# Parted PSUM ring, mixed couples of scores and maxima, and value products by pairs of heads in an attention between two expert layers

## The chip, the cores and the metric

One core of a Trainium2 chip runs the whole program in one launch. The metric is the device time of a run in microseconds (us). Three timed runs of the kernel before gave 1308.31, 1308.95 and 1309.26 us, median 1308.95. The profile is of one further execution.

## The reference, cut to what matters

```python
x = L0_attn_x                                    # (4, 1024, 128) fp32
x = x + 0.5 * ffn(layernorm(x))                  # 8 experts, the best 2 for each of 4096 tokens
x = x + attn(layernorm(x))
x = x + 0.5 * ffn(layernorm(x))                  # the same experts and router

def attn(x):                                     # 16 heads of 8 features; one projection for q, k and v
    qkv = (x @ W_qkv.T).reshape(b, n, 16, 8).transpose(0, 2, 1, 3)
    score = softmax(einsum('bhif,bhjf->bhij', qkv, qkv) / sqrt(8))
    return einsum('bhij,bhjf->bihf', score, qkv).reshape(b, n, 128) @ W_o.T

def ffn(x):                                      # router in fp32, top 2 of 8, softmax over the two gates
    return sum over experts of gate * (clip(x1 * silu(x2)) @ Wo + bo)
```

## The kernel before, in words

There are three stages: the first expert layer, the attention, and the second expert layer. The change lies in the attention alone.

**Tiling.** The attention works through 16 teams: 4 batches by 4 groups of four heads (`TEAM`). A team has two halves of 512 queries each. A half has 8 key tiles of 128 (one key tile of four heads is a unit). A slot is one head, one key tile and 512 queries: its score product fills one PSUM bank (128 keys by 512 queries, fp32). There are 1024 slots, issued in 512 couples. The two scores of a couple contract over 64 rows each, the first over partitions 0 to 63, the second over 64 to 127, so the two can run beside each other in TensorE.

**Row maxima.** Before a half's scores can be made, its row maxima must be known, because they are part of the operands. A maxima unit `n` is two products of 62 rows by 512 keys (a low one on partitions 0 to 61, a high one from partition 64), each into a bank, and one VectorE reduction over both banks. There are 512 such units. The first 18 (`MAX_FIRST`) come before the first score; after that each couple brings one unit, 18 units ahead of the scores. The last 18 couples have none.

**Exponentials.** ScalarE turns each score bank into `att_probs` (8 slots of SBUF).

**Value products.** All value products of a half accumulate in bank 7, cut into four strips of 32 partitions, one for each head of the team. `tensor_values(n, part)` multiplies unit `n` (four heads) with 256 of the 512 queries: four matmuls on the four strips, which the trace shows as eight (fp32). Couple `slot` issues half of the products of unit `slot // 4 - 1`. Part 0 waits until the exponential of the last slot of its unit is done, which is the slot just before the couple.

**PSUM.** Banks 0 to 6 are one ring (class `Ring`): scores (one bank), maxima units (two banks) and the chores' banks take the next free place in the order of issue, and each waits until the holder seven banks back has been read. A maxima unit whose banks are 6 and 0 is not contiguous and is reduced by two instructions (line 1975) in place of one (line 1970).

**Chores.** Everything else of the attention stage is a list of chores by slot, with an order written out by hand (lines 598 to 670). All engines go through the same list: after the couple's own work, each engine does its part of the couple's chores. The chores are: `place` (the maxima's transpose, 31 in the list and one before), `finish` (at a half's end ScalarE copies bank 7 to `att_o_t`, TensorE transposes it, ScalarE copies it back, VectorE takes reciprocals of the sums and GpSimd multiplies), `rows` (the output projection, every fourth team), `prepare` (the next batch's operands) and `route` (the router of the second expert layer). 110 of their steps take a bank, in 102 couples; eight of these couples have two.

**Order on TensorE.** A couple is: first score (line 2264), second score (2268), low maxima (2247), high maxima (2248), value products (2286), chores. The loop is in `tensor_attention`. On VectorE it is: maxima reduction, chores; on ScalarE: two exponentials, chores.

## Time and profile before

| what | us |
|---|---|
| median of three timed runs | 1308.95 |
| the profiled execution's own time | 1308.1 |
| its span, first to last instruction | 1306.4 |
| first expert layer, until the first maxima product | 0 to 335.5 |
| first score to the last exponential | 363.6 to 1060.0 |
| PE busy in the span | 1150.1 |
| VectorE (DVE) busy in the span | 1126.8 |
| ScalarE (ACT) busy in the span | 887.6 |
| GpSimd (POOL) busy in the span | 482.2 |

PE is TensorE's matmul side and PEld its weight loads, which overlap. A matmul's end is modelled, so starts are the safer readings on PE: two matmuls on different rows of the array start within hundredths of a microsecond of each other. "Idle before" is the time an engine stood still ahead of an instruction, and the name behind the arrow is who ended it.

### The profile page before, as it was taken

How to read it: one execution, taken by the hardware profiler on the slowest of the kernel's cores; microseconds unless marked ns; L12 is line 12 of the kernel's file. 1: busy time of each engine (PE TensorE's matmuls, PEld its weight loads, DVE VectorE, ACT ScalarE, POOL GpSimd, SP SyncE). 2: the span in 40 equal slices, each digit the busy share in tenths (PEclk: the TensorE clock that was granted, in tenths of full speed). 3: DMA queues.
4: the chain of work that ended last, by engine and by line, in shares of the span. 5: the costliest groups of instructions: out<-in, count | busy, mean ns of one | idle time of the engine just before them, and what ended most of it. 6: DMA issues, size and time to landing. Idle time of an engine off the chain costs nothing.

```text
span 1306.4 us, 27214 instructions
## 1 busy us (share of the span) xinstructions
PE 1150.1 (88%) x9031; PEld 630.4 (48%) x9031; DVE 1126.8 (86%) x2337; ACT 887.6 (68%) x1879; POOL 482.2 (37%) x545
## 2 busy tenths in 40 slices
PE   3847999888589999999999999999998889999993
PEld 2746888777123223223323223233322258788882
DVE  7877888877899999989998999999999368988885
ACT  1223555555168999898888888898887965455651
POOL 3873547334113000324235313333333117543232
PEclk9999999999679999999999999999999999999997
DMA  8124665564010200002001010001000503554654
GB/s 277 50 70 171 215 212 187 206 215 134 29 50 19 67 6 15 18 18 63 5 27 37 11 32 19 18 26 28 18 5 24 181 31 138 191 204 181 247 199 139
DMA packets 58617, 123.55 MB, mean 95 GB/s; under 512 B 12352, under 2 KB 33826, under 8 KB 58448
## 3 DMA queue, kind: packets, MB, share of 16 engines
q1 hardware_dynamic: 49488, 103.83, 23.1%
q0 software_dynamic: 8704, 16.93, 4.1%
q8 instruction: 75, 1.23, 0.4%
q10 hardware_dynamic: 288, 1.05, 0.2%
q14 instruction: 62, 0.51, 0.1%
HBM read 36.66 MB, written 23.88 MB: 46 GB/s over the span
## 4 chain that ended last, share of the span: by engine, by line
PE 56%; DVE 25%; issue 5%; POOL 5%; ACT 5%; DMA 3%; SPq 1%; DVEq 0%; POOLq 0%; ACTq 0%
PE psum L2286 14%; DVE att_neg_part L1970 12%; PE psum L2264 8%; PE psum L2200 8%; PE psum L2188 7%; PE psum L2190 7%; PE psum L2247 5%; POOL rows_dram L1263 4%; DVE att_neg_part L1975 2%; DMA ffn_block_rows<-rows_dram 2%; DVE ffn_x2c L1911 2%; DVE stats L1604 2%; ACT att_probs L1456 2%; DVE ffn_hidden L1922 1%; PE psum L2309 1%
## 5 line engine op out<-in xcount | busy, mean ns | idle before, releaser
L1456 ACT ACTIVATE att_probs<-psum 128x512 f32<-128x512 f32 x1024 | 554.9, 599 | 59.3 <-PE psum L2268 31.2
L1970 DVE TENSOR_REDUCE att_neg_part<-psum 128x2 f32<-128x1024 f32 x443 | 519.1, 1216 | 33.3 <-PE psum L2248 31.6
L2286 PE MATMUL psum<-att_probs,att_values 128*16 128x256 f32 x4096 | 322.1, 386 | 12.4 <-ACT att_o_t L1471 7.7
L1424 ACT ACTIVATE ffn_silu<-ffn_x2c,ffn_rec 128x256 f32<-128x256 f32 (+1 forms) x320 | 154.6, 487 | 170.1 <-DVE ffn_x2c L1911 170.0
L1279 POOL DMA_INDIRECT y_dram<-ffn_y,ffn_block_rows x144 | 142.4, 989 | 235.0 <-ACT ffn_y L1442 206.5
L2268 PE MATMUL psum<-att_right,att_left 64*128 64x512 f16 x512 | 199.5, 390 | 17.3 <-DVE att_neg_part L1970 13.2
L2247 PE MATMUL psum<-att_right,att_left 62*128 62x512 f16 x512 | 198.4, 388 | 15.6 <-DVE att_neg_part L1970 10.1
L2264 PE MATMUL psum<-att_right,att_left 64*128 64x512 f16 x512 | 199.5, 390 | 8.5 <-DVE att_neg_part L1970 6.8
L2248 PE MATMUL psum<-att_right,att_left 62*128 62x512 f16 x512 | 200.0, 391 | 0.0
L1911 DVE TENSOR_SCALAR ffn_x2c<-psum,ffn_rec 128x256 f32<-128x256 f32 (+1 forms) x320 | 162.8, 513 | 36.7 <-PE psum L2190 33.0
L2188 PE MATMUL psum<-ffn_block_t,ffn_rec 128*128 128x256 f32 (+1 forms) x640 | 179.0, 362 | 1.2 <-ACT ffn_block_t L1375 1.2
L2190 PE MATMUL psum<-ffn_block_t,ffn_rec 128*128 128x256 f32 (+1 forms) x640 | 178.2, 360 | 0.0
L1263 POOL DMA_INDIRECT rows_dram<-rows,place_i x128 | 127.5, 996 | 122.6 <-PE psum L2268 53.6
L2286 PEld LDWEIGHTS psum<-att_probs,att_values 128*16 128x16 f32 x4096 | 69.4, 94 | 192.7 <-issue 134.6
L1922 DVE SCALAR_TENSOR_TENSOR ffn_hidden<-psum,ffn_rec,ffn_silu 128x256 f32<-128x256 f32 (+1 forms) x320 | 144.4, 451 | 19.0 <-ACT ffn_silu L1424 17.0
L2200 PE MATMUL psum<-ffn_hidden,ffn_rec 128*128 128x256 f32 (+1 forms) x640 | 140.6, 363 | 11.8 <-DVE ffn_hidden L1930 11.6
L2264 PEld LDWEIGHTS psum<-att_right,att_left 64*128 64x128 f16 x512 | 47.3, 92 | 203.7 <-ACT att_probs L1456 128.6
L2200 PEld LDWEIGHTS psum<-ffn_hidden,ffn_rec 128*128 128x128 f32 x640 | 111.0, 190 | 32.4 <-DVE ffn_hidden L1930 19.8
L2190 PEld LDWEIGHTS psum<-ffn_block_t,ffn_rec 128*128 128x128 f32 x640 | 117.6, 192 | 13.6
L2188 PEld LDWEIGHTS psum<-ffn_block_t,ffn_rec 128*128 128x128 f32 x640 | 111.9, 192 | 12.2 <-ACT ffn_block_t L1375 1.8
L1192 POOL TENSOR_TENSOR att_attn<-att_o_t,att_inv_sum 128x128 f32<-128x128 f32 x30 | 12.1, 404 | 227.7 <-DVE att_inv_sum L1999 213.0
L1975 DVE TENSOR_REDUCE att_neg_part<-psum 128x1 f32<-128x512 f32 x138 | 88.3, 681 | 4.3 <-PE psum L2248 3.6
(238 smaller groups left out, 1176.6 us busy)
## 6 DMA issues: line engine op xcount, KB each, us to landing
ffn_rec<-record SPq DMA_DIRECT2D x80, 776.5 KB, 3.9
ffn_block_rows<-rows_dram SPq DMA_DIRECT2D x64, 130.0 KB, 3.1
record<-in_L_ffn_W SPq DMA_DIRECT2D x16, 256.0 KB, 6.5
att_left<-q_parts_dram SPq DMA_DIRECT2D x64, 64.0 KB, 2.2
y_dram<-ffn_y,ffn_block_rows POOLq DMA_INDIRECT x144
x_sb<-in_L_attn_x SPq DMA_DIRECT2D x4, 512.0 KB, 7.0
record<-in_L_ffn_Wo SPq DMA_DIRECT2D x8, 256.0 KB, 7.2
rows_dram<-rows,place_i POOLq DMA_INDIRECT x128, 2.4
```

The lines of the kernel that those rows point to most:

```text
L1263: G.indirect_dma_start(rows_dram[k_ffn][:, :], bass.IndirectOffsetOnAxis(ap=r.place_i[:, k, t:t + 1], axis=0), r.rows[:, t, k, :], None).t ...
L1456: S.activation(probs[:, slot % PROBS, :], ring_bank(("score", slot))[:, :], ACT.Exp, scale=unlift).then_inc(att_bank.by_act, 1)
L1911: V.tensor_scalar(mix[k].x2c[:, n % 2, few], chunk_bank[n % 4][:, few], mix[k].rec[:, s, CLIP_LO + c:CLIP_LO + c + 1], mix[k].rec[:, s, CL ...
L1970: last = V.tensor_reduce(out=neg_part[:, h % 2, keys, p::PAIR, t], in_=psum[:, low:high + 1, :], axis=AX.X, op=ALU.max, negate=True)
L2188: TE.matmul(both[:, few], mix[k].rec[:, s, W2 + c * P:W2 + (c + 1) * P], mix[k].block_t[:, m % 2, few], start=True, stop=True)
L2190: TE.matmul(both[:, w1_few], mix[k].rec[:, s, W1 + c * P:W1 + (c + 1) * P], mix[k].block_t[:, m % 2, few], start=True, stop=True).then_inc ...
L2200: last = TE.matmul(y_bank[n % 2][:, few], mix[k].rec[:, s, WO + c * F:WO + (c + 1) * F], mix[k].hidden[:, n % 2, c, few], start=(c == 0), ...
L2247: TE.matmul(bank[low], left[s][PRODUCTS[0], p, q], right[s][PRODUCTS[0], p, k], start=True, stop=True)
L2248: TE.matmul(bank[high], left[s][PRODUCTS[1], p, q], right[s][PRODUCTS[1], p, k], start=True, stop=True).then_inc(maxed, 1)
L2264: TE.matmul(low, left[s][WITH_MAX[0], p, k], right[s][WITH_MAX[0], p, q], start=True, stop=True).then_inc(att_bank.filled, 1)
L2268: TE.matmul(high, left[s][WITH_MAX[1], p, k], right[s][WITH_MAX[1], p, q], start=True, stop=True).then_inc(att_bank.filled, 1)
L2286: last = TE.matmul(value_bank[head * VS:head * VS + VW, q], values[:, b % 2, kt, team * TEAM + head, :], probs[:, (UNIT * n + j) % PROBS, ...
```

## The change

Three things change together in the attention.

1. The ring of seven banks becomes two: banks 0 to 3 for maxima units (two units), banks 4 to 6 for scores and chores. Every maxima unit is contiguous, so line 1975's form is gone.
2. A couple on TensorE becomes: first score, high maxima, low maxima, second score, value products, chores.
3. Value products go by pairs of slots. Pair `m` is slots `2m` and `2m + 1`. It multiplies two heads with all 512 queries: the four strips now hold (odd or even query tile) by (head of the pair), and the bank's two halves of columns hold the two pairs of the team. It is issued in couple `2m + 4` (`VALUE_LAG` = 2). The number of matmuls, and the 256 columns of each, are the same; the moving operand is two runs of 128 columns in place of one of 256. The last multiply of `finish` becomes two, because the layout of the sums has changed.

```diff
-        return (self.at[name] + k) % self.banks
+        return self.first + (self.at[name] + k) % self.banks
...
-        att_bank = Ring(7, semaphore("bank_full"), semaphore("bank_emptied"), maxed, reduced)
+        MAX_BANKS = 2 * PAIR
+        max_bank = Ring(0, MAX_BANKS, None, None, maxed, reduced)
+        att_bank = Ring(MAX_BANKS, 7 - MAX_BANKS, semaphore("bank_full"), semaphore("bank_emptied"), None, None)
...
-                o = o_t[:, half, :].rearrange("p (t j d) -> p t j d", t=HT, j=TEAM)
-                G.tensor_tensor(attn_of(i, half), o[:, :, :, 0:DH],
-                                inv_sum[:, :, :].unsqueeze(3).to_broadcast([P, HT, TEAM, DH]),
-                                ALU.mult).then_inc(finished, 1)
+                o = sums_of(half)
+                for j in range(PAIR):
+                    last = G.tensor_tensor(attn_of(i, half, j), o[:, j, :, :, 0:DH], inverse_of_sums(j), ALU.mult)
+                last.then_inc(finished, 1)
...
-                    if slot >= PROBS and slot % UNIT == 0:
-                        S.wait_ge(valued, slot // UNIT - PROBS // UNIT + 1)
+                    if slot >= PROBS and slot % PAIR == 0:
+                        S.wait_ge(valued, (slot - PROBS) // PAIR + 1)
...
-            if high == low + 1:
-                last = V.tensor_reduce(out=neg_part[:, h % 2, keys, p::PAIR, t], in_=psum[:, low:high + 1, :],
-                                       axis=AX.X, op=ALU.max, negate=True)
-            else:
-
-                for k, where in enumerate((low, high)):
-                    last = V.tensor_reduce(out=neg_part[:, h % 2, keys, PAIR * k + p, t:t + 1], in_=bank[where],
-                                           axis=AX.X, op=ALU.max, negate=True)
-            last.then_inc(reduced, 1)
+            V.tensor_reduce(out=neg_part[:, h % 2, keys, p::PAIR, t], in_=psum[:, low:high + 1, :],
+                            axis=AX.X, op=ALU.max, negate=True).then_inc(reduced, 1)
...
-                tensor_scores(slot)
-                for n in max_units(slot + 1):
-                    tensor_row_max(n)
-                if slot >= UNIT:
-                    tensor_values(slot // UNIT - 1, slot % UNIT // 2)
+                tensor_scores(slot, max_units(slot + 1))
+                if slot // PAIR >= VALUE_LAG:
+                    tensor_values(slot // PAIR - VALUE_LAG)
                 for chore in chores[slot] + chores[slot + 1]:
                     tensor_chore(*chore)
-            for part in range(2):
-                tensor_values(NSCORES // UNIT - 1, part)
+            for m in range(NSCORES // PAIR - VALUE_LAG, NSCORES // PAIR):
+                tensor_values(m)
...
             TE.matmul(low, left[s][WITH_MAX[0], p, k], right[s][WITH_MAX[0], p, q],
                       start=True, stop=True).then_inc(att_bank.filled, 1)
+            for n in beside:
+                tensor_row_max(n, (1, 0))
             for emptied in att_bank.empty_before(("score", slot + 1)):
                 TE.wait_ge(*emptied)
...
-            q = slice(part * HALF // 2, (part + 1) * HALF // 2)
-            for j, head in enumerate(HEAD_OF):
-                last = TE.matmul(value_bank[head * VS:head * VS + VW, q], values[:, b % 2, kt, team * TEAM + head, :],
-                                 probs[:, (UNIT * n + j) % PROBS, q],
-                                 start=(kt == 0 and part == 0), stop=(kt == BT - 1 and part == 1))
-            if part == 1:
-                last.then_inc(valued, 1)
+            TE.wait_ge(*att_bank.emptied(("score", PAIR * m + 1)))
+            for odd in range(2):
+                for h in range(PAIR):
+                    g = odd * PAIR + h
+                    queries = probs[:, (PAIR * m + h) % PROBS, :].rearrange("p (c o q) -> p c o q", o=2, q=P)[:, :, odd, :]
+                    last = TE.matmul(value_bank[g * VS:g * VS + VW, p * HALF // 2:(p + 1) * HALF // 2],
+                                     values[:, b % 2, kt, team * TEAM + HEAD_OF[PAIR * p + h], :], queries,
+                                     start=(kt == 0 and p == 0), stop=(kt == BT - 1 and p == 1))
+            last.then_inc(valued, 1)
```

## Rows read from the trace of the kernel before

**Rows 1.** Windows: span, PE, PEld, DVE, ACT, POOL busy, clock, DMA.
```profile
363.00:1024.00 661.00, 624.58 (x6178) 200.09 (x6178) 620.68 (x875) 580.88 (x1137) 200.97 (x230) 0.99 0.09 25
```
**Rows 2.** Page, costliest groups: busy and mean ns, then idle before.
```profile
L1970 DVE TENSOR_REDUCE att_neg_part<-psum 128x2 f32<-128x1024 f32 x443 | 519.1, 1216 | 33.3 <-PE psum L2248 31.6
...
L1192 POOL TENSOR_TENSOR att_attn<-att_o_t,att_inv_sum 128x128 f32<-128x128 f32 x30 | 12.1, 404 | 227.7 <-DVE att_inv_sum L1999 213.0
L1975 DVE TENSOR_REDUCE att_neg_part<-psum 128x1 f32<-128x512 f32 x138 | 88.3, 681 | 4.3 <-PE psum L2248 3.6
```
**Rows 3.** Waits of DVE and of PE, 363 to 1024: us, times, longest.
```profile
DVE att_neg_part L1970 <- PE psum L2248: 29.9, 51, 1.1
DVE att_neg_part L1975 <- PE psum L2248: 3.6, 6, 1.0
...
PE psum L2286 <- ACT att_o_t L1471: 6.9, 20, 0.5
```
**Rows 4.** Timeline of DVE over one plain half: start, us, what.
```profile
456.52 1.23 DVE L1970 TENSOR_REDUCE att_neg_part<-psum 128x2 f32<-128x1024 f32 x1 [0.45 <-PE psum L2248]
...
459.11 1.28 DVE L1975 TENSOR_REDUCE att_neg_part<-psum 128x1 f32<-128x512 f32 x2
460.31 4.61 DVE L1970 TENSOR_REDUCE att_neg_part<-psum 128x2 f32<-128x1024 f32 x4
464.83 1.28 DVE L1975 TENSOR_REDUCE att_neg_part<-psum 128x1 f32<-128x512 f32 x2
466.02 6.88 DVE L1970 TENSOR_REDUCE att_neg_part<-psum 128x2 f32<-128x1024 f32 x6
472.81 1.29 DVE L1975 TENSOR_REDUCE att_neg_part<-psum 128x1 f32<-128x512 f32 x2
```
**Rows 5.** Timeline of PE over one couple late in that half.
```profile
467.28 0.39 PE L2264 MATMUL psum<-att_right,att_left 64*128 64x512 f16 x1
...
467.30 0.39 PE L2268 MATMUL psum<-att_right,att_left 64*128 64x512 f16 x1
...
467.50 0.38 PE L2247 MATMUL psum<-att_right,att_left 62*128 62x512 f16 x1
...
467.83 0.62 PE L2286 MATMUL psum<-att_probs,att_values 128*16 128x256 f32 x8
...
468.39 0.39 PE L2264 MATMUL psum<-att_right,att_left 64*128 64x512 f16 x1
```
**Rows 6.** Timeline of ACT and PE over a half's end.
```profile
452.94 0.59 ACT L1471 COPY att_o_t<-psum 128x512 f32<-128x512 f32 x1
...
453.63 0.62 PE L2286 MATMUL psum<-att_probs,att_values 128*16 128x256 f32 x8 [0.38 <-ACT att_o_t L1471]
...
455.28 0.66 PE L2309 MATMUL psum<-identity,att_o_t 128*128 128x128 f32 x4
...
455.87 0.39 PE L2264 MATMUL psum<-att_right,att_left 64*128 64x512 f16 x1
...
455.97 0.59 ACT L1476 COPY att_o_t<-psum 128x512 f32<-128x512 f32 x1 [0.28 <-PE psum L2309]
```
**Rows 7.** Timeline around a couple with two chores.
```profile
518.30 0.59 ACT L1483 COPY att_xh_t<-psum 128x512 f32<-128x512 f32 x1 [0.28 <-PE psum L2315]
...
518.30 0.39 PE L2264 MATMUL psum<-att_right,att_left 64*128 64x512 f16 x1
...
518.89 0.37 PE L2247 MATMUL psum<-att_right,att_left 62*128 62x512 f16 x1 [0.20 <-ACT att_xh_t L1483]
...
519.32 1.23 DVE L1970 TENSOR_REDUCE att_neg_part<-psum 128x2 f32<-128x1024 f32 x1 [0.57 <-PE psum L2248]
```
**Rows 8.** Timeline of ACT: half ends, the last half without maxima.
```profile
472.05 0.59 ACT L1471 COPY att_o_t<-psum 128x512 f32<-128x512 f32 x1
...
1019.03 0.59 ACT L1471 COPY att_o_t<-psum 128x512 f32<-128x512 f32 x1
...
1037.77 0.59 ACT L1471 COPY att_o_t<-psum 128x512 f32<-128x512 f32 x1
```

More of the change, by code:

```diff
@@ L55, with __init__ @@
 class Ring:
-    def __init__(self, banks, filled, by_act, maxed, reduced):
-        self.banks = banks
+    def __init__(self, first, banks, filled, by_act, maxed, reduced):
+        self.first, self.banks = first, banks
         self.filled, self.by_act, self.maxed, self.reduced = filled, by_act, maxed, reduced
@@ L591, in max_banks @@
         def max_banks(n):
-            return [att_bank.bank(("max", n), k) for k in range(PAIR)]
+            return [max_bank.bank(("max", n), k) for k in range(PAIR)]
         PLACINGS = 2 * NTEAM
@@ L1467, in scalar_chore @@
                 i, half = which
-                S.wait_ge(valued, i * UNITS + (half + 1) * BT)
+                S.wait_ge(valued, i * PAIRS + (half + 1) * PAIRS // 2)
                 if i:
@@ L1998, in vector_chore @@
                         V.wait_ge(finished, 2 * i + half)
-                    V.reciprocal(inv_sum[:, :, :], o[:, :, :, DH]).then_inc(sums_inverted, 1)
+                    V.reciprocal(inv_sum[:, :], all_sums(half)).then_inc(sums_inverted, 1)
                 else:
                     V.wait_ge(finished, 2 * i + half)
-                    settle(V.reciprocal(inv_sum[:, :, :], o[:, :, :, DH]))
-                    V.tensor_tensor(attn_of(i, half), o[:, :, :, 0:DH],
-                                    inv_sum[:, :, :].unsqueeze(3).to_broadcast([P, HT, TEAM, DH]),
-                                    ALU.mult).then_inc(finished, 1)
+                    settle(V.reciprocal(inv_sum[:, :], all_sums(half)))
+                    for j in range(PAIR):
+                        last = V.tensor_tensor(attn_of(i, half, j), o[:, j, :, :, 0:DH], inverse_of_sums(j), ALU.mult)
+                    last.then_inc(finished, 1)
             elif what == "rows" and step == 2 and which[0] == B - 1:
@@ L2014, in vector_chore, with attn_of, sums_of, all_sums @@
                 vector_prepare(which, step, part)
-        def attn_of(i, half):
+        def attn_of(i, half, j):
             team = i % TEAMS
             where = attn[:, half * HT:(half + 1) * HT, team * TEAM * DH:(team + 1) * TEAM * DH]
-            return where.rearrange("p t (j d) -> p t j d", j=TEAM)
+            return where.rearrange("p t (h j d) -> p j t h d", h=PAIR, j=PAIR)[:, j, :, :, :]
+        def sums_of(half):
+            return o_t[:, half, :].rearrange("p (j t h d) -> p j t h d", j=PAIR, t=HT, h=PAIR)
+        def all_sums(half):
+            return o_t[:, half, :].rearrange("p (s d) -> p s d", d=VS)[:, :, DH]
+        def inverse_of_sums(j):
+            sums = inv_sum[:, :].rearrange("p (j t h) -> p j t h", j=PAIR, t=HT)[:, j, :, :]
+            return sums.unsqueeze(3).to_broadcast([P, HT, PAIR, DH])
         def vector_prepare(b, step, part):
@@ L2241, in tensor_row_max, with tensor_max_half, tensor_scores @@
                 TE.wait_ge(rights_in[s], rights_before(i))
-            for emptied in att_bank.empty_before(("max", n)):
+            for emptied in max_bank.empty_before(("max", n)):
                 TE.wait_ge(*emptied)
-            low, high = max_banks(n)
-            q = slice((g * HT + t) * P, (g * HT + t + 1) * P)
-            k = slice(keys * HALF, (keys + 1) * HALF)
-            TE.matmul(bank[low], left[s][PRODUCTS[0], p, q], right[s][PRODUCTS[0], p, k], start=True, stop=True)
-            TE.matmul(bank[high], left[s][PRODUCTS[1], p, q], right[s][PRODUCTS[1], p, k],
-                      start=True, stop=True).then_inc(maxed, 1)
-        def tensor_scores(slot):
+            for k in halves:
+                tensor_max_half(n, k, k == halves[-1])
+        def tensor_max_half(n, k, whole):
+            i, g, p, t, keys = max_of(n)
+            s = i % OPERANDS
+            q = slice((g * HT + t) * P, (g * HT + t + 1) * P)
+            seen = slice(keys * HALF, (keys + 1) * HALF)
+            product = TE.matmul(bank[max_banks(n)[k]], left[s][PRODUCTS[k], p, q], right[s][PRODUCTS[k], p, seen],
+                                start=True, stop=True)
+            if whole:
+                product.then_inc(maxed, 1)
+        def tensor_scores(slot, beside):
             i, at = divmod(slot, TURN)
@@ L2269, in tensor_scores, with tensor_values @@
                       start=True, stop=True).then_inc(att_bank.filled, 1)
-        def tensor_values(n, part):
+        def tensor_values(m):
+            n, p = divmod(m, UNIT // PAIR)
             i, u = divmod(n, UNITS)
@@ L2275, in tensor_values @@
             b, team = divmod(i, TEAMS)
-            if part == 0:
+            if p == 0:
                 TE.wait_ge(*when_emptied(("prepare", b, 15)))
```

15 lines of the change are left out of this document (8 added, 7 removed).

## The prediction
> **What bounds the kernel now.** I read the windows by stage first. From the first score to the last maxima reduction (363 to 1024 us) the span is 661.0 us, and DVE is busy for 620.7 of them, PE for 624.6 and ACT for 580.9 [rows 1]. PE's figure contains modelled ends, so it says little; DVE's is 94% and ends are real. The waits of DVE in the same stretch say where most of the other 40.3 us are: 29.9 + 3.6 = 33.5 us in 57 waits, all of them for the high maxima product, line 2248 [rows 3]. So DVE is the bound, and what it loses it loses to TensorE being late with a maxima unit.
>
> The timeline of a plain half (no `rows`, `prepare` or `route`) shows how close the engines stand. Sixteen couples go from one copy of bank 7 at 452.94 [rows 6] to the next at 472.05 [rows 8]: 19.11 us. DVE's reductions follow each other without a gap but for one wait of 0.45 us [rows 4]. Four contiguous ones take 464.83 - 460.31 = 4.52 us, so 1.13 us each; six take 472.81 - 466.02 = 6.79, again 1.13. A split unit takes 460.31 - 459.11 = 1.20 or 466.02 - 464.83 = 1.19.
>
> PE is nearly as full. In one couple the second score starts at 467.30, the low maxima at 467.50, the value products at 467.83, the next first score at 468.39 [rows 5]. From score to value products is 0.53, from there to the next score 0.56, so PE needs 0.53 + 0.56 = 1.09 to 1.10 us for a couple, 0.03 less than DVE. The last half has no maxima, and there the same copies are 1037.77 - 1019.03 = 18.74 us apart [rows 8]: that is what ACT and PE allow when DVE asks for nothing. A perfect decoupling would so win 19.11 - 18.74 = 0.37 us in a plain half.
>
> Where does the one wait of a half come from? PE's value products wait for the copy of bank 7, which ends at 452.94 + 0.59 = 453.53 (call it Tc), and start at 453.63. Then PE runs without a pause: a couple, the transposes at 455.28, and the score of the couple after that at 455.87, Tc + 2.34 [rows 6]. Its maxima are ready for DVE at 456.52, Tc + 2.99 [rows 4]. DVE had a little less than two units in hand, and PE has spent 0.46 on the copy and 0.59 on the transposes. It is TensorE's own work that is late, not its waits for exponentials: among PE's waits in the stretch the value products are held 6.9 us by the copy [rows 3], and no wait of comparable size for `att_probs` stands beside it.
>
> **The change part by part.**
>
> *Contiguous maxima.* 138 / 2 = 69 of the 512 units are split [rows 2]. Each saves 1.195 - 1.13 = 0.065 us on DVE (by busy time, 2 x 0.681 - 1.216 = 0.146, but neighbours overlap at their ends, so the spacing of starts is the price): 69 x 0.065 = 4.5 us. This lies on the engine that sets the pace. The part of it that falls just ahead of a wait only makes that wait longer. With 33.5 us of waits in 57 places, I count 85% as kept: -3.8 us. Bounds: 0 (all swallowed) and -10.1 (0.146 each).
>
> *Two rings, maxima.* By the lines of `empty_before`, a unit's banks needed before: the reduction of the unit two back and, for the second bank, the exponential of slot - 2. Now they need the reduction two back only. But the first score, which stands ahead of them on TensorE in both kernels, needs the exponential of slot - 3 in both. So in DVE's pace nothing moves: reduction two back ends, + 0.15 the second score started before (467.15 to 467.30, the ends being 466.02 + 1.13 k) [rows 4, 5], and now the high maxima does. The second row group is then free 0.20 later for the second score, and the value products follow at the same + 0.68. After Tc, too, the low maxima is the second pair in either order, 0.2 after the first score: DVE's Tc + 2.99 stays. Cost 0, gain 0.
>
> *Two rings, chores.* Eight couples take two chore banks; in the couple behind them a maxima unit had to wait for the reduction just before it: it starts at 518.89, and DVE stood idle for 0.57 us [rows 7]. This goes. What is late next is the second score: with three banks it needs the bank of the first chore, whose copy ends at 518.30 + 0.59 = 518.89. It would have come at 518.30 + 0.2 = 518.5, and starts near 518.97. So DVE gets its unit 0.37 earlier, but the value products behind the second score come 0.07 later (0.2 + 0.1 of order and latency against what the low maxima needed before), and the next unit with them. Net +0.07 x 8 = +0.6. Bounds: +0.45 each (3.6 us, if PE had no wait there before) and -0.57 each (-4.6).
> A single chore holds one of three banks. Behind a `finish`, the first score two couples on needs the copy that ends at 455.97 + 0.59 = 456.56, and TensorE comes to it at 455.87 + 1.10 = 456.97 [rows 6]: 0.4 to spare, less the 0.1 that a release takes. Cost 0 in the 94 couples with one chore; if that cover is gone, PE loses what is missing each time.
>
> *Order within a couple.* The pairs still use opposite row groups (0 to 63 beside 64 to 127), so I take the same spacing of 0.20 to 0.22 between pairs. The trace of before has no pair of score and maxima side by side. Bounds: 0 and +0.2 per pair, which is the full start-to-start time when nothing overlaps [rows 5].
> The Trainium skill (TensorE: Matmul & The Clock Gate, Part 3, "What overlaps and what doesn't") says that a weight load overlaps a running matmul only where the row group differs. The new order alternates low, high, low, high as the old one did, so by that page too the sum has 0 here; no run so far shows a mixed pair.
>
> *Value products.* Eight matmuls of 256 columns on four strips, as before. They wait for exponentials of slot - 3 and older in place of slot - 1; that frees TensorE where ACT is late, but such waits are not in the list [rows 3]. The wait for the copy of bank 7 is in the same couple (last pair of a half in couple at + 2, first of the next in at + 4). Gain 0 to -2. The moving operand in two runs has no row; I take 0.56 as before. Bounds: 0 and a doubled 0.56, which would be the end of any gain.
> The Trainium skill (PSUM — Partial Sum Buffer, Specifications) says that any non-contiguous access pattern slows matmuls. It speaks of PSUM, where the output stays one run of 256; were it to hold for what is read, this change would be the slower one. No run so far shows it.
>
> *Last pairs, finish.* At the very end half of the last products no longer waits for the last exponential, but the copy after it stands behind a table load on ACT: 0. GpSimd's second multiply adds at most 0.40 us in each of 30 `finish` chores, and GpSimd sat idle 227.7 us ahead of them [rows 2]: 0. ACT's wait for old values is relaxed: 0. No DMA moves. The 18 couples at the end lose the bank reserve of seven, but are paced by ACT, and TensorE is freer: -0.3.
>
> **Sum.** -3.8 + 0.6 - 0.3 = -3.5 us. The profiled execution took 1308.1 us (its span of 1306.4 and 1.7 around it), so 1304.6 for such an execution. The median of the timed runs is 0.85 higher: 1308.95 - 3.5 = 1305.4 us.
>
> **The rivals.**
>
> A, DVE's waits shrink. If the looser order (value products two pairs behind, maxima ahead of the second score) lets TensorE build up a lead, each half falls from DVE's pace to the 18.74 of ACT: 0.37 x 28 halves = 10.4 us, 1308.95 - 10.4 = 1298.5. For it: DVE waits for PE alone, in 57 places. Against it: in those places PE is shown working without a pause, and a lead grows by 0.03 us a couple at most.
>
> B, slower: a score waits for a chore's copy. With three banks the chore's bank comes round in the second couple. The reserve I computed is 0.3 to 0.4 us behind a `finish`. It decides from the point where the copy ends over 0.3 us later against TensorE than in [rows 6]; then PE, with only 0.03 us of slack a couple, hands it on to DVE. At 0.1 us in each of the 94 couples and the full 0.45 in the eight doubles: 9.4 + 3.6 - 3.8 = +9.2, 1318.2 us; half of that is 1313.
>
> C, slower: TensorE's couple gets longer, through the mixed pairs or the two-run reads. The point is 0.03 us a couple; every 0.01 beyond costs 494 x 0.01 = 4.9 us. At +0.05 it would be +10 - 3.8, some 1315; with one pair not overlapping (+0.2) it would be 1308.95 + 494 x 0.17 = 1393.
>
> D, nothing shows: the 4.5 us of splits end in front of waits, 1308.
>
> **How the numbers follow.** The forecast gets 0.44 (its own range 1303 to 1307.5), A 0.20, B 0.14, C 0.09, D 0.13. What a measurement here can tell from no change is about 0.2%, 2.6 us, so faster means below 1306.3. The forecast lies below that in about 0.31 of its 0.44, and the rest is no change. Faster: 0.31 + 0.20 = 0.51; same: 0.13 + 0.13 = 0.26; slower: 0.14 + 0.09 = 0.23. The range leaves out the upper part of B and C and the lower part of A: 1296 to 1312.
>
> **What would show it.** Line 1975's form is gone, 512 reductions, DVE busy in the stretch down by 5 to 10 us. A plain half takes 18.9 to 19.0 us between copies of bank 7, with one wait of DVE of 0.4 to 0.5. The 0.57 behind double chores is gone, and the wait after it is longer. Value products show 0.56 to the next first score. The forecast is wrong if DVE's waits for line 2247 or 2248 fall well under 30 us in total (A), if scores wait for ACT's chore copies in more than the eight places (B), or if a couple on PE without waits takes over 1.13 us (C).

## The result, and the profile after

The changed kernel takes 1300.68 us (median of 4 runs, 1299.04 to 1302.95) beside 1308.97 us for the kernel before in the same session: a ratio of 0.9947, interval 0.9933 to 0.9961. Timed again in a later session (the last run below) the ratio was 0.9955, interval 0.9942 to 0.9968, or -6.0 us. Faster by 6 to 8 us, then, where -3.5 was forecast: 1300.68 lies in the stated range of 1296 to 1312, which holds "no change" as well, and 4.7 us under the forecast.

The page and the windows of the changed kernel first. They answer to [rows 1, 2]: there is one form of reduction, 512 times, and the busy time of all of them is 594.7 us where 519.1 + 88.3 = 607.4 stood. The last reduction starts at 1017.12 us where it started at 1023.91. DVE is busy for 616.7 us up to 1018, for 620.7 up to 1024 before: 4 us less, where 5 to 10 were foretold.

```profile
L1973 DVE TENSOR_REDUCE att_neg_part<-psum 128x2 f32<-128x1024 f32 x512 | 594.7, 1213 | 35.5 <-PE psum L2259 32.1
```
```profile
363.00:1018.00 655.00, 625.01 (x6190) 175.82 (x6188) 616.74 (x809) 580.79 (x1138) 205.53 (x261) 0.99 0.09 25
```

The waits of DVE and PE in that stretch (total us, times, longest) answer to [rows 3]. In this kernel line 2259 is both maxima products, 2277 the first score, 2283 the second, 2304 the value products, 1475 the copy of bank 7. DVE still waits for nothing but maxima: 30.4 us in 47 places for 33.5 in 57 (30.8 in 48 in the second profile of this kernel, below). PE's 6.5 us ahead of the value products are its stands for the copy.

```profile
DVE att_neg_part L1973 <- PE psum L2259: 30.4, 47, 1.4
```
```profile
PE psum L2304 <- issue: 6.5, 19, 0.4
```

DVE over a plain half (timeline: start, us, what), as in [rows 4]. Fourteen reductions run without a split, 1.13 apart, and the one wait is what it was, 0.46.

```profile
456.44 15.93 DVE L1973 TENSOR_REDUCE att_neg_part<-psum 128x2 f32<-128x1024 f32 x14
472.82 1.23 DVE L1973 TENSOR_REDUCE att_neg_part<-psum 128x2 f32<-128x1024 f32 x1 [0.46 <-PE psum L2259]
```

PE and ACT late in that half and over its end, as in [rows 5, 6]. The pair of a score and a maxima product starts within 0.04 us, the next pair 0.23 later. Behind the copy of bank 7 the value products stand 0.31 for the copy; then PE runs a couple in 470.50 to 471.59 = 1.09 us, and reaches the score behind the transposes at 472.18, the copy's end (469.84) + 2.34. That is to the hundredth what [rows 6] have.

```profile
463.33 0.39 PE L2277 MATMUL psum<-att_right,att_left 64*128 64x512 f16 x1
463.37 0.56 PE L2259 MATMUL psum<-att_right,att_left 62*128 62x512 f16 x2
463.60 0.38 PE L2283 MATMUL psum<-att_right,att_left 64*128 64x512 f16 x1
463.90 0.63 PE L2304 MATMUL psum<-att_probs,att_values 128*16 128x256 f32 x8
...
469.25 0.59 ACT L1475 COPY att_o_t<-psum 128x512 f32<-128x512 f32 x1
...
469.94 0.62 PE L2304 MATMUL psum<-att_probs,att_values 128*16 128x256 f32 x8 [0.31 <-issue]
470.50 0.39 PE L2277 MATMUL psum<-att_right,att_left 64*128 64x512 f16 x1
...
471.04 0.62 PE L2304 MATMUL psum<-att_probs,att_values 128*16 128x256 f32 x8
471.59 0.66 PE L2326 MATMUL psum<-identity,att_o_t 128*128 128x128 f32 x4
472.18 0.39 PE L2277 MATMUL psum<-att_right,att_left 64*128 64x512 f16 x1
```

Behind two chores, as in [rows 7]: the maxima start beside the first score, the second score stands 0.64 us behind it for the chore's copy, and DVE has one wait of 1.37.

```profile
515.20 0.39 PE L2277 MATMUL psum<-att_right,att_left 64*128 64x512 f16 x1
515.21 0.60 PE L2259 MATMUL psum<-att_right,att_left 62*128 62x512 f16 x2
...
515.84 0.39 PE L2283 MATMUL psum<-att_right,att_left 64*128 64x512 f16 x1
...
518.44 1.23 DVE L1973 TENSOR_REDUCE att_neg_part<-psum 128x2 f32<-128x1024 f32 x1 [1.37 <-PE psum L2259]
```

What the chores cost DVE is read from starts. In the changed kernel the three units ahead of the wait begin at 513.36, and the unit behind it at 518.44: 5.08 us.

```profile
513.36 3.71 DVE L1973 TENSOR_REDUCE att_neg_part<-psum 128x2 f32<-128x1024 f32 x3
```

In the kernel before, the same three units and both waits take from 516.39 to 521.51, 5.12 us (the wait of [rows 7] lies inside).

```profile
516.39 2.35 DVE L1970 TENSOR_REDUCE att_neg_part<-psum 128x2 f32<-128x1024 f32 x2
...
521.51 1.23 DVE L1970 TENSOR_REDUCE att_neg_part<-psum 128x2 f32<-128x1024 f32 x1 [0.96 <-PE psum L2248]
```

ACT in the last half without maxima, as in [rows 8], and under it the row of the kernel before that is needed beside it: the half takes 17.76 us (the copy before stands at 1012.25) for 18.74, because 20 exponentials take 10.11 us for 10.85.

```profile
1020.03 10.11 ACT L1460 ACTIVATE att_probs<-psum 128x512 f32<-128x512 f32 x20
1030.01 0.61 ACT L1475 COPY att_o_t<-psum 128x512 f32<-128x512 f32 x1
```
```profile
1027.04 10.85 ACT L1456 ACTIVATE att_probs<-psum 128x512 f32<-128x512 f32 x20
```

**A ruler.** ACT copies bank 7 once in each half, 32 times. The starts of these copies cut the attention into 31 pieces that can be compared between kernels to hundredths. In the table: start of the first copy, the 29 halves behind it, the last two (which have no maxima, or few), and one plain half (the fifth).

| kernel | first copy | 29 halves | last two | plain half |
|---|---|---|---|---|
| before | 388.81 | 630.22 | 42.35 | 19.11 |
| after | 386.82 | 625.43 | 40.87 | 18.97 |
| after, again | 388.35 | 625.52 | 40.59 | 18.97 |
| value products alone | 388.58 | 628.76 | 39.73 | 19.11 |
| parted rings alone | 388.35 | 631.01 | 42.62 | 19.25 |
| parted rings, mixed order | 387.41 | 627.37 | 42.62 | 18.97 |
| after, with splits | 387.79 | 627.45 | 40.50 | 19.10 |

Between first and last copy the change is worth 672.57 - 666.30 = 6.3 us (6.5 in the second profile): 4.8 (4.7) in the 29 halves, 1.5 (1.8) in the last two. The first copy is another matter: the two profiles of the same changed kernel have it 2.0 and 0.5 us earlier than before. Part of that lies ahead of the attention, where the kernels do not differ: the first maxima product starts at 335.48 us before, at 335.21 and 336.14 in the two profiles after. From it to the first copy it is 53.33 us before, 51.61 and 52.21 after. In this stretch the granted clock differs too. In the windows of 368 to 372 us (column ahead of the last two) it is 0.50, which is the 1.2 GHz level, for the whole window before and in the second profile, and it rises within the window in the first. In the next 4 us it is 0.73 before, 0.92 in the second profile and 1.00 in the first.

```profile
368.00:372.00 4.00, 4.00 (x25) 0.56 (x24) 3.26 (x3) 1.97 (x4) 0.00 (x0) 0.50 0.00 0
```
```profile
368.00:372.00 4.00, 4.00 (x35) 0.69 (x36) 3.05 (x4) 2.54 (x6) 0.00 (x0) 0.67 0.00 0
```
```profile
368.00:372.00 4.00, 4.00 (x25) 0.56 (x23) 3.19 (x4) 2.96 (x6) 0.00 (x0) 0.50 0.00 0
```

So of the 8.3 us between the first two medians some 6.4 are the change in the middle of the kernel. The rest is not shown to be the change's. Some of it differs from one execution to the next; whether the new order also shortens the start cannot be told from the clock's part in it, with one profile of the kernel before.

### The profile page after: what moved, and what is told of

The parts are those of the page before. It is cut to its first block, busy times and chain, and to the rows that moved or that the text cites. A ratio compares the mean times of both kernels' runs of the same rounds, so it can differ in the third digit from the quotient of the medians.

```text
span 1297.3 us, 26926 instructions
## 1 busy us (share of the span) xinstructions
PE 1152.7 (89%) x9031; PEld 607.3 (47%) x9031; DVE 1122.0 (86%) x2270; ACT 886.0 (68%) x1879; POOL 486.7 (38%) x575
## 4 chain that ended last, share of the span: by engine, by line
PE 60%; DVE 25%; POOL 5%; issue 5%; ACT 2%; DMA 2%; SPq 1%; DVEq 0%; POOLq 0%; ACTq 0%
PE psum L2304 15%; DVE att_neg_part L1973 13%; PE psum L2277 8%; PE psum L2208 8%; PE psum L2196 7%; PE psum L2198 7%; PE psum L2259 6%; POOL rows_dram L1267 4%; DVE ffn_x2c L1915 2%; DVE stats L1608 2%; DMA ffn_block_rows<-rows_dram 1%; DVE ffn_hidden L1926 1%; PE psum L2326 1%; PE psum L2283 1%; ACT ffn_silu L1428 1%
## 5 line engine op out<-in xcount | busy, mean ns | idle before, releaser
L1973 DVE TENSOR_REDUCE att_neg_part<-psum 128x2 f32<-128x1024 f32 x512 | 594.7, 1213 | 35.5 <-PE psum L2259 32.1
L2259 PE MATMUL psum<-att_right,att_left 62*128 62x512 f16 x1024 | 288.4, 395 | 36.4 <-DVE att_neg_part L1973 34.3
L2277 PE MATMUL psum<-att_right,att_left 64*128 64x512 f16 x512 | 198.8, 388 | 0.0
L2283 PE MATMUL psum<-att_right,att_left 64*128 64x512 f16 x512 | 194.9, 381 | 0.2
L1197 POOL TENSOR_TENSOR att_attn<-att_o_t,att_inv_sum 128x64 f32<-128x64 f32 x60 | 16.4, 293 | 225.4 <-DVE att_inv_sum L1996 211.2
L2259 PEld LDWEIGHTS psum<-att_right,att_left 62*128 62x128 f16 x1024 | 52.3, 94 | 67.6 <-DVE att_neg_part L1973 64.5
L1230 POOL TENSOR_TENSOR rstd<-shifted,minus_half 128x8 f32<-128x8 f32 (+1 forms) x18 | 27.6, 1533 | 78.3 <-DVE shifted L1655 41.3
```

What stands on the lines that cost most here:

```text
L1973: V.tensor_reduce(out=neg_part[:, h % 2, keys, p::PAIR, t], in_=psum[:, low:high + 1, :], axis=AX.X, op=ALU.max, negate=True).then_inc(red ...
L2259: product = TE.matmul(bank[max_banks(n)[k]], left[s][PRODUCTS[k], p, q], right[s][PRODUCTS[k], p, seen], start=True, stop=True)
L2277: TE.matmul(low, left[s][WITH_MAX[0], p, k], right[s][WITH_MAX[0], p, q], start=True, stop=True).then_inc(att_bank.filled, 1)
L2283: TE.matmul(high, left[s][WITH_MAX[1], p, k], right[s][WITH_MAX[1], p, q], start=True, stop=True).then_inc(att_bank.filled, 1)
```

## The experiments

**Value products alone** (part 3 of the change on the kernel before: one ring of seven, old order, splits kept).

```diff
-                if slot >= UNIT:
-                    tensor_values(slot // UNIT - 1, slot % UNIT // 2)
+                if slot // PAIR >= VALUE_LAG:
+                    tensor_values(slot // PAIR - VALUE_LAG)
```


> The kernel before with the new value products alone (pairs, two behind); one ring of seven banks, old order of the couple, 69 split reductions. Theory: a half that DVE paces gains nothing from it (plain half 19.1 us between copies of bank 7), because what is late there is TensorE's own work; the last half without maxima falls from 18.74 to about 17.8 us, since there the exponentials were held by the loop over the value products, and some 0.5 us come after it. In all -1 to -2 us, 1307 to 1308. Rival (looser order gives TensorE a lead everywhere): plain halves 18.8 or less, -5 us or more.

Measured: 1305.3 us (11 runs) beside 1307.01, ratio 0.9980 (0.9968 to 0.9992). The ruler says -1.5 us in the 29 halves and -2.6 in the last two, and nothing in a plain half. Where the first comes from is seen behind a `rows` chore. The kernel before:

```profile
697.39 2.07 ACT L1456 ACTIVATE att_probs<-psum 128x512 f32<-128x512 f32 x4
...
698.14 0.39 PE L2248 MATMUL psum<-att_right,att_left 62*128 62x512 f16 x1
...
698.62 0.62 PE L2286 MATMUL psum<-att_probs,att_values 128*16 128x256 f32 x8
```

The same place in the kernel with the new value products:

```profile
697.23 0.39 PE L2261 MATMUL psum<-att_right,att_left 62*128 62x512 f16 x1
697.54 0.62 PE L2302 MATMUL psum<-att_probs,att_values 128*16 128x256 f32 x8
```

Before, the value products stand 0.48 us behind the maxima, for the second exponential behind the chore's copy; with the new lag 0.31, which is the plain spacing. That is 0.17 us where a chore's copy delays the exponentials. No wait was named: between the modelled end of the maxima (698.14 + 0.39) and the value products lie only 0.09 us; it is found in the spacing of starts. The trace before has this spacing of 0.48 at nine places between the first copy and the last halves, the trace of this run at two, both while the granted clock is at 0.50 (near 984 and 994 us). Six of the nine halves they lie in are 0.23 to 0.25 us shorter in this run, which is 1.4 of the 1.5 us; the other three are not. The 0.07 us that such a half gains beyond 0.17 was not traced.

In the last half the 20 exponentials take 9.65 us. Before they took 10.85. A loop held them: score, two exponentials, value products that wait for them, next score. The list of waits of the kernel before names it, over 1019 to 1038 us, where the same list of this run has no wait for an exponential:

```profile
PE psum L2286 <- ACT att_probs L1456: 1.9, 6, 0.4
```

One of the six, with the score that stands in the queue behind it:

```profile
1029.19 0.63 PE L2286 MATMUL psum<-att_probs,att_values 128*16 128x256 f32 x8 [0.39 <-ACT att_probs L1456]
1029.74 0.39 PE L2264 MATMUL psum<-att_right,att_left 64*128 64x512 f16 x1
```

The exponential of that score starts at 1030.17, 0.75 us behind the one ahead of it, where the 20 of this run start some 0.48 apart.

**Parted rings alone** (part 1; old order on TensorE, old value products).

```diff
-            for emptied in att_bank.empty_before(("max", n)):
+            for emptied in max_bank.empty_before(("max", n)):
```


> The kernel before with the parted rings alone; old order and old value products. Theory: all 69 split units become contiguous, 69 x 0.065 = 4.5 us on DVE, which sets the pace: about 1304.5, plain half 18.97, last half unchanged at 18.7. Rival (three banks for scores and chores make scores wait for chore copies): part or all of the 4.5 us is given back, 1307 or more.

Measured: 1308.9 us (12 runs), ratio 1.0007 (0.9997 to 1.0017): the expected gain is not there, and this was my largest miss in kind. A plain half has become longer, 19.25 us, although no split is left. The couple behind the `place` chore shows it; PE in this kernel (PEld is the weight load of the second score, with what it waited for):

```profile
479.84 0.39 PE L2266 MATMUL psum<-att_right,att_left 64*128 64x512 f16 x1
...
480.09 0.09 PEld L2270 LDWEIGHTS psum<-att_right,att_left 64*128 64x128 f16 x1 [0.17 <-ACT att_probs L1458]
...
480.10 0.39 PE L2270 MATMUL psum<-att_right,att_left 64*128 64x512 f16 x1
480.10 0.39 PE L2249 MATMUL psum<-att_right,att_left 62*128 62x512 f16 x1
...
480.32 0.38 PE L2250 MATMUL psum<-att_right,att_left 62*128 62x512 f16 x1
```

and in the changed kernel:

```profile
476.77 0.39 PE L2277 MATMUL psum<-att_right,att_left 64*128 64x512 f16 x1
476.77 0.60 PE L2259 MATMUL psum<-att_right,att_left 62*128 62x512 f16 x2
...
477.03 0.39 PE L2283 MATMUL psum<-att_right,att_left 64*128 64x512 f16 x1
```

The second score starts 0.26 us behind the first in both. In the old order that is a stand, since two scores without a wait start within 0.04 us of each other ([rows 5] have 0.02), and the maxima stand behind it. In the mixed order it is nearly the plain spacing of 0.23, and the maxima are already issued. DVE's fourteen reductions take 16.21 us in place of 15.93.
What the score waits for is an exponential and not a chore's copy: the chore holds one of the three banks, so the score needs the bank of the second score before it, whose exponential ends at 480.04. In this trace 66 second scores come more than 0.1 us behind their first (380 to 1015 us); 58 of them start within 0.08 us of the end of an exponential, 8 within that of the end of a chore's copy. So it is not the prediction's rival B as it was put, but a near relative, and the mixed order is what keeps it away from DVE.

**Parted rings and mixed order** (parts 1 and 2, old value products).

```diff
-                tensor_scores(slot)
-                for n in max_units(slot + 1):
-                    tensor_row_max(n)
+                tensor_scores(slot, max_units(slot + 1))
```


> Parted rings and the mixed couple, old value products. Theory: as the rings alone in the middle (plain half 18.97); at the cold start, where TensorE runs at 1.2 GHz, the maxima no longer stand behind a second score that waits, so up to 1.5 us less in the first copy of bank 7: 1303 to 1304.5. Rival (mixed pairs overlap less): TensorE's couple over 1.13 us and slower than the rings alone by 5 us or more.

Measured: 1304.18 us (8 runs), ratio 0.9980 (0.9969 to 0.9990). The ruler: -2.85 us in the 29 halves, +0.27 in the last two. The mixed order is worth 631.01 - 627.37 = 3.6 us once the rings are parted. Together with the value products alone, the parts come to -4.1 - 2.6 = -6.7 us between first and last copy; the whole has -6.3 to -6.5. In all they add to within 0.4 us, but not by place: in the 29 halves the whole has 4.7 to 4.8 where the parts sum to 4.3, and in the last two 1.5 to 1.8 where they sum to 2.4.

**The changed kernel with its splits back**: the 69 units that were split before are reduced by two instructions again, over the same banks.

```diff
+            if n in SPLIT_UNITS:
+                for k, where in enumerate((low, high)):
+                    last = V.tensor_reduce(out=neg_part[:, h % 2, keys, PAIR * k + p, t:t + 1], in_=bank[where],
+                                           axis=AX.X, op=ALU.max, negate=True)
```


> The changed kernel with the same 69 maxima units reduced by two instructions as before (banks stay contiguous). Theory: +69 x 0.065 = +4.5 us on 1300.7, so 1305.2, plain half 19.1. Rival (the splits were hidden and the gain comes from the looser order): 1301 to 1302, plain half 18.97.

Measured: 1303.5 us (11 runs), ratio 0.9975 (0.9964 to 0.9985), on the chip where the three above ran (the changed kernel itself was not timed there). The ruler: 2.0 us more in the 29 halves, 0.13 = 2 x 0.065 in a plain one, nothing in the last two. So the contiguous maxima are worth 2.0 us, not 3.8. In the plain halves the price holds exactly; in nine of the 29 halves, all of them with chores, the splits cost 0.01 us or nothing. As I read it, DVE waits behind a long chore anyway.

**First value pair of a half one couple later.** At this point my theory was that TensorE's stand at the copy of bank 7 is the start of DVE's one wait of a half.

```diff
-                if slot // PAIR >= VALUE_LAG:
-                    tensor_values(slot // PAIR - VALUE_LAG)
+                m = slot // PAIR - VALUE_LAG
+                if m >= 0:
+                    if m and (m - 1) % (PAIRS // 2) == 0:
+                        tensor_values(m - 1)
+                    if m % (PAIRS // 2):
+                        tensor_values(m)
```


> The changed kernel, but the first value pair of each half is issued one couple later, together with the second pair, so TensorE no longer stands at the value products until bank 7 is copied; nothing else moves. Theory: DVE's one wait of a plain half (0.45 us) comes from TensorE's 0.3 to 0.5 us at the copy plus its 0.59 us of transposes. Without the first, the score behind the transposes starts 0.5 us earlier against the copy, the wait shrinks to 0 to 0.15, a plain half falls from 18.97 to 18.5 to 18.7 us, and some 28 halves give 8 to 12 us: 1289 to 1293. Rival (ACT or the exponentials pace the half, TensorE's lead does not matter): 18.9 or more, 1299 to 1301.

Measured: 1305.2 us (12 runs), ratio 0.9986 (0.9977 to 0.9995): slower than the changed kernel, where 8 to 12 us less were expected. The rival's 1299 to 1301 missed too. The 29 halves take 628.53 us for 625.43. The half's end on PE and DVE:

```profile
471.15 0.39 PE L2263 MATMUL psum<-att_right,att_left 62*128 62x512 f16 x2 [0.35 <-DVE att_neg_part L1973]
...
471.71 1.06 PE L2308 MATMUL psum<-att_probs,att_values 128*16 128x256 f32 x16
472.70 0.66 PE L2330 MATMUL psum<-identity,att_o_t 128*128 128x128 f32 x4
...
473.93 1.23 DVE L1973 TENSOR_REDUCE att_neg_part<-psum 128x2 f32<-128x1024 f32 x1 [0.57 <-PE psum L2263]
```

TensorE does not stand for the copy any more, but there is nothing that it may do instead: the banks of the maxima hold two units, both are full, and it stands for DVE. Then two value pairs and the transposes come in one piece, and DVE's wait is 0.57 for 0.46. Work moved past a stand helps only if a free bank takes the work that moves up.

**Start with a warm clock**, on the kernel before and on the changed one: each of the first maxima products is issued three times (the same factor of 3 in both kernels), so that TensorE is busier ahead of 364 us.

```diff
-                tensor_row_max(n)
+                tensor_row_max(n, 3)
```


> The kernel before with each product of the first 18 maxima units computed three times, so that TensorE is busy ahead of the first score. Theory: of the 2.0 us by which the changed kernel reached its first copy of bank 7 earlier, about 1.3 are the granted clock rising earlier (it rose near 374 us before, near 371 after). If TensorE is at 2.4 GHz from the first score on, DVE's three waits of 0.73, 0.73 and 0.56 there go: first copy near 387, 1307 of 1309. Rival (the start is paced by DVE or by the order, not by the clock): first copy stays at 388.5 to 389.

> The changed kernel with the same threefold first products. Theory: its one wait of 0.8 us at the start goes, first copy near 386; the distance of the two warm kernels at the first copy is 0.5 to 0.8 us, not 2.0. Rival: the distance stays at 2.0, as the order makes it.

Measured: 1307.58 us (11 runs, ratio 0.9997, 0.9988 to 1.0007) and 1301.97 us (6 runs, 0.9960, 0.9948 to 0.9972). The added products delay the start themselves (first copies at 391.11 and 388.44 us), so neither tells what the clock costs there. The windows of 368 to 372 us show the clock at 0.68 in the first (where it falls to 0.50 in the next window) and full in the second. With the clock full there the changed kernel is no earlier than its second profile with the clock at 0.50 (388.44 and 388.35). The two first copies lie 2.67 us apart, more than either expectation had (0.5 to 0.8, or 2.0), but with different clocks. So the start stays open.

```profile
368.00:372.00 4.00, 3.21 (x18) 0.62 (x18) 4.00 (x5) 2.28 (x4) 0.00 (x0) 0.68 0.00 0
```
```profile
368.00:372.00 4.00, 2.95 (x31) 0.72 (x27) 4.00 (x4) 3.53 (x8) 0.00 (x0) 1.00 0.01 4
```

**Value products one pair behind** in place of two.

```diff
-    VALUE_LAG = 2
+    VALUE_LAG = 1
```


> The changed kernel with value pairs one couple behind in place of two. Theory: the loop score, two exponentials, value products, next score is back in every couple; the last half without maxima goes from 17.8 back to 18.5 or more and the halves with rows and prepare lose 0.2 to 0.3 us each: 1302.5 to 1304. Rival (it is the pairs, not the lag, that won): 1300 to 1301, last half 17.8.

Measured: 1337.09 us (5 runs), ratio 1.0224 (1.0211 to 1.0238); a plain half takes 20.18 us, the last half 20.04. The expectation missed by 33 us. The half's end:

```profile
476.50 0.59 ACT L1475 COPY att_o_t<-psum 128x512 f32<-128x512 f32 x1
477.19 0.63 PE L2304 MATMUL psum<-att_probs,att_values 128*16 128x256 f32 x8 [1.48 <-ACT att_o_t L1475]
```

The last pair of a half is now one couple ahead of the first pair of the next, and the copy, queued behind two exponentials, comes between them. TensorE stands 1.48 us for it; with a lag of two it is 0.31. So the lag buys two things: the exponentials of a couple, and a couple's time for the copy.

**The copy of bank 7 earlier**: ScalarE copies between the two exponentials of its couple and not behind both.

```diff
+                    if slot == first:
+                        for chore in chores[first + 1]:
+                            if chore[0] == "finish" and chore[2] == 0:
+                                scalar_chore(*chore)
```


> The changed kernel, with one thing moved: ScalarE copies bank 7 (the value products of the last half) between the two exponentials of its couple and not behind both. My theory is that each half of the changed kernel is now set by a loop: end of the copy, value products, transposes, score and maxima, and DVE's one wait of 0.45 us. The copy then starts as soon as the last value pair is done, some 0.18 us earlier, TensorE's stand of 0.31 to 0.39 us at the first value pair shrinks by as much, DVE's wait at the end of a half falls to 0.25 to 0.3 and a plain half from 18.97 to about 18.8 us: 28 halves x 0.15 to 0.18 = 4 to 5 us less than the changed kernel, a ratio to before of about 0.991. The rival: the second exponential of that couple comes 0.35 us later (a copy of 0.59 ahead of it), and the first score three slots on and the value pair behind it lose as much as the copy gave: same time as the changed kernel or up to 3 us more.

Measured: 1302.61 us (10 runs), ratio 0.9961 (0.9948 to 0.9974), beside 1301.61 for the changed kernel in the same session. The rival holds.

```profile
471.84 0.63 PE L2309 MATMUL psum<-att_probs,att_values 128*16 128x256 f32 x8 [0.18 <-issue]
472.39 0.39 PE L2282 MATMUL psum<-att_right,att_left 64*128 64x512 f16 x1
...
472.78 0.39 PE L2288 MATMUL psum<-att_right,att_left 64*128 64x512 f16 x1
473.10 0.62 PE L2309 MATMUL psum<-att_probs,att_values 128*16 128x256 f32 x8
```

The stand falls from 0.31 to 0.18 (0.18 less was expected). But the exponential behind the copy is late, the second score stands for its bank (0.39 behind the first where 0.23 is the spacing), and from one value pair to the next it is 1.26 us where the changed kernel has 471.04 - 469.94 = 1.10: 0.13 won, 0.16 lost. DVE's wait is 0.49 us, not less than before. A plain half takes 19.01 us for 18.97.

**All banks for the last 18 couples**, and **both** edits together.

```diff
+            if slot == NSCORES - 2 * MAX_FIRST:
+                assert not max_units(slot + 1)
+                att_bank.widen(max_bank)
```


> The changed kernel, with one thing more: for the last 18 couples, which have no maxima, the scores use all seven banks again. My theory is that with three banks the last two halves lose 0.4 us + 0.7 us (parting the ring alone took them from 18.74 and 23.61 to 18.96 and 23.66, and the value products alone gave 17.36 and 22.37 where the whole change has 17.76 and 23.11), because a score waits for an exponential three slots back. So the last two halves go from 40.87 to about 39.7 us: 1.1 us less than the changed kernel, a ratio of about 0.9938, and no other half changes. The rival, that the exponentials themselves set the end, gives no difference at all.

> The changed kernel with both: the copy of bank 7 between the two exponentials, and all seven banks for the scores of the last 18 couples. The two lie in different halves, so my theory adds them: 5 to 6 us less than the changed kernel, a ratio of about 0.990. If the early copy costs the exponentials behind it what it gives, about 1 us less than the changed kernel.

> The changed kernel as it is, on the same chip as the three variants of it, to compare them with: a ratio to before of 0.9947 as in the first result (interval 0.9933 to 0.9961), a plain half of 18.97 us, DVE's wait at the end of it 0.45 us.

| kernel (same session) | us (runs) | ratio | 29 halves | last two |
|---|---|---|---|---|
| copy earlier | 1302.61 (10) | 0.9961 (0.9948 to 0.9974) | 625.96 | 40.54 |
| all banks at the end | 1301.8 (6) | 0.9961 (0.9947 to 0.9976) | 625.50 | 39.80 |
| both | 1302.44 (5) | 0.9967 (0.9954 to 0.9980) | 625.96 | 39.49 |
| the changed kernel | 1301.61 (5) | 0.9955 (0.9942 to 0.9968) | 625.52 | 40.59 |

The bank theory is right about the end and small: the last half falls from 17.75 to 17.36 us, the length it has with the value products alone, and 20 exponentials take 9.70 us.

```profile
1021.45 9.70 ACT L1473 ACTIVATE att_probs<-psum 128x512 f32<-128x512 f32 x20
```

0.8 us in the last two halves (0.4 of them in the one without maxima, which repeats to 0.01 us) are plain on the ruler and lost in the spread of the timed runs (2 to 7 us from lowest to highest). Both together have 39.49 us there. The expected ratios of 0.9938 for all banks and 0.990 for both were not met. The changed kernel itself came out as expected, with its plain half of 18.97 us and a ratio of 0.9955 for 0.9947. No variant is shown to beat the changed kernel.

## Why the prediction was right, and where it was off

**Contiguous maxima** (-3.8): the term is right in kind and half the size, -2.0. The price of 0.065 stands; what failed is "I count 85% as kept". I had put that share on 33.5 us of waits in 57 places without walking through a half with long chores. In nine halves the time saved is swallowed, which had been my rival D for all of it.

**Two rings, maxima** (0) and **order within a couple** (0): right for the two together. A plain half is 19.11 - 0.13 (two splits) = 18.98, measured 18.97. The score beside the maxima costs nothing: PE needs 1.09 us a couple, as [rows 5] have it, under rival C's mark of 1.13. The rule of the Trainium skill (TensorE: Matmul & The Clock Gate, Part 3) that a load overlaps a running matmul in another row group was read as "0 here"; the trace agrees, 0.04 us from the score at 463.33 to the maxima beside it. What I had not seen is that the two edits need each other: parting alone costs 0.8 us in the 29 halves where its splits alone would have saved 2.0.

**Two rings, chores** (+0.6): the steps came as told. The 0.57 is gone, the second score stands 0.64 us for the chore's copy (518.97 - 518.30 = 0.67 was forecast), the next wait is longer. But it is one wait of 1.37 where two of 0.57 and 0.96 stood, and by starts the three units take 5.08 us for 5.12: -0.04 in place of +0.07 each. Rival B's mark, scores that wait for copies in more than eight places, was hardly passed: in the changed kernel ten second scores start right behind the end of a chore's copy, 0.64 us (six), 0.4 (two) and 0.31 (two) behind their first. What I had left out is the wait for an exponential that parting brings behind a chore, 0.26 us behind a `place`. With the old order parting cost more than the splits gave, and my reserve of 0.3 to 0.4 us was worked out for the copies of `finish` alone.

**Value products** (0, bounds 0 to -2): this step failed. Alone they gave -1.5 us in the middle and -2.6 at the end, -4.1 in all; put on top of the parted rings and the mixed order, -3.7 to -3.9. I wrote that waits for exponentials "are not in the list [rows 3]"; they are 0.17 us at nine places, below what the list names, behind chores whose copy delays ACT. Reads in two runs cost nothing, 0.56 to the next score as before (469.94 to 470.50). What the Trainium skill says of non-contiguous access in PSUM (PSUM — Partial Sum Buffer, Specifications) was not put to the test: what is read in two runs here lies in SBUF.

**Last pairs, finish** (-0.3): -1.5 to -1.8 us. The step that failed stands ahead of the sum: "that is what ACT and PE allow when DVE asks for nothing" of the 18.74 us. It was no floor: six waits for exponentials, 1.9 us, stand in that half, and [rows 3] end at 1024 us, early in it. The exponentials had room, and the lag opened the loop that held them: 17.36 with seven banks, 17.76 with three. Rival A, built on 18.74 as the floor, fell as it was put: DVE's waits are 30.4 and 30.8 us, not under the mark of 30 that I had set for it, and its wait in a plain half is untouched. What it said of a looser order holds behind the chores alone.

**The sum.** By the ruler -6.3 to -6.5: -2.0 splits, -4.1 value products, and the rest, some -0.3, for double chores and what the parts give each other (an estimate by difference). Forecast -3.5. The error is one of size: +1.8 on the splits, -3.8 on the value products with the last halves, and -0.9 on the rings' chores, where -0.04 at each of eight double chores, as read at one of them, would make the -0.3. That the forecast came as near as it did is luck in part, since the first of these errors runs against the other two. The plain half, on which the argument rested, came out to 0.01 us; the halves with chores and the last ones, which I had not walked through, made the difference. The first session's 8.3 us exceed the ruler by some 2, the later session's 6.0 do not; that rest belongs to no term.

**Still open.** What sets the one wait of 0.46 us in a plain half. Taking TensorE's stand away (one couple later) and shortening it (earlier copy) both met the next resource: two maxima units, then a score bank. A third maxima unit would need two banks more than there are, and was not tried.

## What to carry to other kernels

The critical stage's list of waits names only waits long enough to show: compare the spacing of the same instruction in a plain place and behind each kind of disturbance, since 0.17 us at nine places never showed as a wait, and the halves around them made up the 1.5 us. A stretch without the bounding engine's work shows a floor only if no queue in it closes a loop of waits; ask for the waits of that very stretch before you call it what the others allow. Here the answer would have been one line, 1.9 us of waits for exponentials. And where a shared buffer is parted, look at what stands in the same queue behind the user that got fewer places: the order of issue has to change with it, or the parting costs more than it frees.

## What the runs showed of the hardware

A value pair of eight matmuls on four column strips takes 0.56 us to the next row-paired product whether its moving operand is one run of 256 columns or two of 128. A product of 64 rows and one of 62 rows on the other half of the array start 0.04 us apart and cost no more than two alike. GpSimd's multiply takes 0.293 us for 128x64 and 0.404 for 128x128, so halving it costs 0.18 us a time, here under an idle wait of 15 us. The granted clock's rise at the start comes at different times in two executions of one kernel (0.67 and 0.50 in 368 to 372 us), and the stretch from the first maxima product to the first copy beside it took 51.61 and 52.21 us.
